# The way into the expert loop of an attention and mixture-of-experts kernel: an expert number loaded earlier on TensorE, three activation and residual pieces re-ordered, token loads in three buffers

## The reference

```python
x = x + xattn(layernorm(x), ctx)           # 16 heads of 32, 112 queries, causal mask
h = layernorm(x).reshape(T, H)
scores = softmax(h @ gate_weight.T)        # E = 8 experts
w, idx = top_k(scores, 2)
gu = einsum('th,efh->tef', h, gate_up)     # F = 352, gate and up together 704 wide
act = silu(gu[..., :F]) * gu[..., F:]
y = einsum('tef,te,ehf->th', act, combine(w, idx), down)
sgu = h @ shared_gate_up.T                 # a shared expert, Fs = 704
y = y + (silu(sgu[:, :Fs]) * sgu[:, Fs:]) @ shared_down.T
out = x + y
```

## Time and profile before

| | |
|---|---|
| time, median of 3 runs | 344.97 us (343.78 to 345.1) |
| the profiled execution's own time | 346.77 us |
| its span, first to last instruction | 345.0 us |
| TensorE busy | 327.2 us, 95% of the span |
| VectorE busy | 267.9 us, 78% |
| ScalarE busy | 233.1 us, 68% |
| GpSimd busy | 133.2 us, 39% |
| chain that ended last | PE 69%, ACT 10%, DVE 8%, DMA 6%, issue 3% |

### The profile page before, as it was taken

One profiled execution on the slowest core, in us unless ns is written; L12 is line 12 of the kernel. 1 busy time (PEld: TensorE's weight loads), 2 busy tenths in 40 slices (PEclk: granted clock), 3 DMA queues, 4 the chain that ended last, 5 costly groups with the idle time before them and its releaser, 6 DMA issues.

```text
span 345.0 us, 7024 instructions
## 1 busy us (share of the span) xinstructions
PE 327.2 (95%) x2285; PEld 281.6 (82%) x2285; DVE 267.9 (78%) x675; ACT 233.1 (68%) x582; POOL 133.2 (39%) x144
## 2 busy tenths in 40 slices
PE   7999979999999998999999899999999999999990
PEld 6898858777776786889898778889988998998980
DVE  4889757999936348855487999999998989999930
ACT  4666988999953232312326578898898889889830
POOL 4335464777844000164400007765742321231231
PEclk9999987999999999999999999999999999999996
DMA  7999300000002799994689953564455456455333
GB/s 232 378 341 379 110 1 3 3 2 1 3 2 95 289 357 327 430 327 152 217 253 236 299 179 82 96 135 101 84 117 130 84 89 138 103 89 120 71 42 50
DMA packets 31795, 53.01 MB, mean 154 GB/s; under 512 B 7440, under 2 KB 14992, under 8 KB 30736
## 3 DMA queue, kind: packets, MB, share of 16 engines
q1 hardware_dynamic: 27616, 43.34, 38.4%
q0 software_dynamic: 4144, 9.23, 14.9%
HBM read 32.22 MB, written 16.92 MB: 142 GB/s over the span
## 4 chain that ended last, share of the span: by engine, by line
PE 69%; ACT 10%; DVE 8%; DMA 6%; issue 3%; POOL 2%; POOLq 1%; SPq 0%; DVEq 0%; ACTq 0%
PE bank L554 26%; PE bank L877 21%; ACT prob L1038 5%; PE bank L901 5%; DMA out<-y_sb,dest 3%; PE bank L615 3%; PE bank L905 2%; PE bank L915 2%; PE bank L776 2%; PE bank L763 2%; PE bank L911 2%; DVE gu_parts L1279 2%; PE bank L546 2%; PE bank L626 1%; DMA w_sg<-sguT 1%
## 5 line engine op out<-in xcount | busy, mean ns | idle before, releaser
L533 POOL DMA_INDIRECT out<-y_sb,dest x21 | 38.4, 1830 | 114.9 <-DMA out<-y_sb,dest 68.1
L1279 DVE TENSOR_TENSOR gu_parts<-w_gu,gu_parts 128x704 fp32r<-128x704 f32 x84 | 77.0, 951 | 0.8 <-ACT gu_parts L993 0.4
L993 ACT ACTIVATE gu_parts<-w_gu 128x704 fp32r x84 | 66.2, 793 | 13.9 <-PE bank L877 12.3
L877 PE MATMUL bank<-gu_parts,xsT_hi 128*128 128x352 f32 x328 | 70.0, 335 | 1.4 <-DVE xsT_lo L1279 0.9
L877 PEld LDWEIGHTS bank<-gu_parts,xsT_hi 128*128 128x128 f32 x328 | 53.7, 188 | 8.8 <-issue 8.7
L877 PE MATMUL bank<-gu_parts,xsT_lo 128*128 128x352 f32 x164 | 39.7, 323 | 0.0
L554 PE MATMUL bank<-x2T_hi,w_sg_lo 128*128 128x512 f32 (+1 forms) x88 | 32.7, 372 | 0.2
L430 POOL TENSOR_TENSOR prob<-prob,rrow 112x448 f32<-112x448 f32 x30 | 27.5, 935 | 12.3 <-DVE rrow L1329 12.3
L554 PE MATMUL bank<-x2T_hi,w_sg_hi 128*128 128x512 f32 (+1 forms) x88 | 32.0, 363 | 0.0
L554 PE MATMUL bank<-x2T_lo,w_sg_hi 128*128 128x512 f32 (+1 forms) x88 | 31.9, 363 | 0.0
L506 POOL DMA_INDIRECT xs_dram<-x2n,slot_i x14 | 14.8, 1057 | 37.9 <-DVE eid L1574 33.9
(11 more groups left out here) (216 smaller groups left out, 830.8 us busy)
## 6 DMA issues: line engine op xcount, KB each, us to landing
w_gu<-guT SPq DMA_DIRECT2D x8, 1408.0 KB
xs_dram<-no_row SPq DMA_DIRECT2D x1, 5460.0 KB, 19.6
xs_in<-xs_dram SPq DMA_DIRECT2D x21, 256.0 KB, 4.5
w_dn<-dnT SPq DMA_DIRECT2D x8, 512.0 KB, 5.4
act_w<-act_e SPq DMA_DIRECT2D x19, 176.0 KB, 2.7
w_sg<-sguT SPq DMA_DIRECT2D x10, 256.0 KB, 5.4
w_dn<-dnT SPq DMA_DIRECT2D x8, 192.0 KB, 6.1
w_sd<-sdnT SPq DMA_DIRECT2D x5, 256.0 KB, 6.0
```

Source lines behind the costliest of these rows:

```text
L533: pool.indirect_dma_start(out=out[:, :], out_offset=bass.IndirectOffsetOnAxis(ap=dest[:, i, 0:1], axis=0), in_=y_sb[i % 2][:, :], in_offse ...
L877: ins = pe.matmul(dst[:, 0:F], xsT[x_][:, c, :], gu2[w_][:, c, f0:f0 + F], start=c == 0 and n == 0, stop=c == C - 1 and n == 2)
L993: act.activation(dst, src, ACT.Copy).then_inc(s[sem], 1)
L1279: dve.tensor_tensor(lo_, src, hi_.bitcast(F32), ALU.subtract).then_inc(s[sem], 1)
```

## The change

There are six edits, and all lie at the entrance of the expert loop or in it.

1. TensorE loads the number of the first tile's expert (`e_first`) ahead of `shared_down(ND-1, 0)`, together with the wait for `pos`, and no longer between chunk 0 and chunk 1 of `gate_up(1)`. The other tiles load theirs where they did.
2. TensorE waits for `xs_lo` of tiles 1 to 20 ahead of the third pair of products of chunk 0, and no longer ahead of the first.
3. VectorE's last three additions are spread: two stood ahead of `gu_lo` of tile 1 and one behind `dn_lo(0)`. Now the first is behind `gu_lo(1, 0)`, the second behind `gu_lo(1, 2)` and the third behind `aT_lo(0)`.
4. `xs_in` is three buffers. Token tile 2 has one of its own (in the place of `y_sb0`), the even tiles from 4 on one at the end of the shared region, and tiles 0, 1 and the odd ones the old one. `load_x(2)` is issued right behind the late down weights.
5. On SP's queue `act_words` of tile 0 stands ahead of the first `start_sum`. The second `start_sum` stands behind `act_words` of tile 1. `load_x(i+3)` stands behind `act_words` of tile i, where `load_x(i+2)` stood ahead of it.
6. On ScalarE `put_y(18)` stands ahead of `dn_hi(19)` and not behind it.

```diff
--- before.py
+++ after.py
@@ -164,6 +164,7 @@
     actT_split = pair(loop, "actT_split", [P, 2, P])
     actT_plain_at = loop[0]
     actT_plain = m.inside(loop, "actT_plain", [P, P])
+    y0_at = loop[0]
     y_sb = [m.inside(loop, "y_sb0", [P, H])]
 
     parts = [shared_at, shared_end]
@@ -182,7 +183,8 @@
                nc.alloc_sbuf_tensor_at("dn_last_lo", [P, (E - 1) * H], F32R, offset=dn_last_lo_at))
 
     sb = lambda name, shape, dtype=F32: m.inside(small, name, shape, dtype)
-    xs_in = sb("xs_in", [P, XW])
+    xs_in = [sb("xs_in", [P, XW]), nc.alloc_sbuf_tensor_at("xs_in1", [P, H], F32, offset=shared_end - 4 * H),
+             nc.alloc_sbuf_tensor_at("xs_in2", [P, H], F32, offset=y0_at)]
     no_row = nc.alloc_sbuf_tensor_at("no_row", [P, XW], F32, offset=act_p_at)
     ident_f = sb("ident_f", [P, P], F32R)
     negmax = sb("negmax", [SQ, R, C])
@@ -259,8 +261,10 @@
 
         "sg ssil sact sact_hi sact_lo sdn sres "
 
-        "xin Tx xs_hi xs_lo gu_hi gu_lo dn_hi dn_lo eg esil eact actw Ta aT_hi aT_lo aT dn_last_hi dn_last edn_split edn ey yst").split()
+        "xin0 xin1 xin2 Tx xs_hi xs_lo gu_hi gu_lo dn_hi dn_lo eg esil eact actw Ta aT_hi aT_lo aT dn_last_hi dn_last edn_split edn ey yst").split()
     s = {n: nc.alloc_semaphore(f"s_{n}") for n in names}
+
+    token_buffer = lambda i: 2 if i == 2 else 1 if i > 2 and i % 2 == 0 else 0
 
     with nc.Block() as block:
 
@@ -341,7 +345,7 @@
 
 
             def load_x(i):
-                sp.dma_start(xs_in[:, 0:H], xs_dram[bass.ds(i * P, P), 0:H]).then_inc(s["xin"], 16)
+                sp.dma_start(xs_in[token_buffer(i)][:, 0:H], xs_dram[bass.ds(i * P, P), 0:H]).then_inc(s[f"xin{token_buffer(i)}"], 16)
 
             for e in range(0, 2):
                 load_gu(e, s["wegu"])
@@ -374,28 +378,32 @@
             for e in range(E - n_late, E):
                 load_dn(e, s["wedn_late"])
 
+            load_x(2)
+
             def start_sum(n0, n1):
                 sp.dma_start(tiles_of(out, n0, n1), xres[:, n0:n1, :]).then_inc(s["ysum0"], 16)
 
+            def act_words():
+
+                sp.dma_start(act_w[:, :], act_e[:, :]).then_inc(s["actw"], 16)
+
+            sp.wait_ge(s["eact"], 1)
+            act_words()
+            sp.wait_ge(s["Tx"], 2)
+            load_x(3)
             sp.wait_ge(s["sres"], NX * ND - XB[1] + 1)
             start_sum(0, BLK + 1)
-            sp.wait_ge(s["Tx"], 2)
-            load_x(2)
-
-            def act_words():
-
-                sp.dma_start(act_w[:, :], act_e[:, :]).then_inc(s["actw"], 16)
-
-            sp.wait_ge(s["eact"], 1)
-            act_words()
-            sp.wait_ge(s["sres"], NX * ND)
-            start_sum(BLK + 1, NX)
             for i in range(1, NT - 2):
-                sp.wait_ge(s["Tx"], i + 2)
-                load_x(i + 2)
                 sp.wait_ge(s["Ta"], i)
                 sp.wait_ge(s["eact"], i + 1)
                 act_words()
+                if i == 1:
+                    sp.wait_ge(s["sres"], NX * ND)
+                    start_sum(BLK + 1, NX)
+                    sp.wait_ge(s["sdn"], NX * ND)
+                if i + 3 < NT:
+                    sp.wait_ge(s["Tx"], i + 2)
+                    load_x(i + 3)
 
             sp.wait_ge(s["yst"], 16 * NT)
             sp.wait_ge(s["ysum0"], 16 * 3)
@@ -770,11 +778,12 @@
 
 
             def t_x(i, bank_=S[2]):
-                pe.wait_ge(s["xin"], 16 * i + 16)
+                own = token_buffer(i)
+                pe.wait_ge(s[f"xin{own}"], 16 * sum(token_buffer(n) == own for n in range(i + 1)))
                 pe.wait_ge(s["idf"], 1)
                 for c in range(C):
                     ins = pe.transpose(bank_[:, c * P:(c + 1) * P].bitcast(F32R),
-                                       xs_in[:, c * P:(c + 1) * P].bitcast(F32R), ident_f[:, :])
+                                       xs_in[token_buffer(i)][:, c * P:(c + 1) * P].bitcast(F32R), ident_f[:, :])
                 ins.then_inc(s["Tx"], 1)
 
             out_bank = (B, CC, D, A)
@@ -860,6 +869,8 @@
             pe.wait_ge(s["sact"], NBLK * (ND - 1) + 1)
             t_x(0, S[1])
             shared_gu(ND, 1)
+            pe.wait_ge(s["pos"], 3)
+            e_first = pe.value_load(eid[0:1, 0:1], min_val=0, max_val=E - 1)
             shared_down(ND - 1, 0)
             shared_down(ND - 1, 1, slice(0, XB[1] - 1))
 
@@ -868,11 +879,14 @@
 
                 if chunks[0] == 0:
                     pe.wait_ge(s["xs_hi"], i + 1)
-                    pe.wait_ge(s["xs_lo"], i + 1)
+                    if i == 0:
+                        pe.wait_ge(s["xs_lo"], 1)
                 for c in chunks:
                     pe.wait_ge(s["gu_hi"], C * i + c + 1)
                     pe.wait_ge(s["gu_lo"], C * i + c + 1)
                     for n, (x_, w_) in enumerate(((0, 1), (0, 0), (1, 0))):
+                        if c == 0 and x_ == 1 and i > 0:
+                            pe.wait_ge(s["xs_lo"], i + 1)
                         for dst, f0 in ((S[0], 0), (S[1], F)):
                             ins = pe.matmul(dst[:, 0:F], xsT[x_][:, c, :], gu2[w_][:, c, f0:f0 + F],
                                             start=c == 0 and n == 0, stop=c == C - 1 and n == 2)
@@ -956,11 +970,10 @@
             t_x(1)
             shared_down(ND - 1, 1, slice(XB[1] - 1, None))
             pe.wait_ge(s["sres"], NX * ND - XB[1] + 1)
-            pe.wait_ge(s["pos"], 3)
             for i in range(1, NT - 1):
                 pe.wait_ge(s["eact"], i)
                 gate_up(i, range(1))
-                e = expert(i - 1, lowest=int(i > SPLIT_FROM))
+                e = expert(i - 1, lowest=int(i > SPLIT_FROM)) if i > 1 else e_first
                 gate_up(i, range(1, C - 1))
                 if i == NT - 2:
                     e_last = [expert(n, lowest=1) for n in (NT - 2, NT - 1)]
@@ -1251,8 +1264,10 @@
                     act.wait_ge(s["wedn"], 16 * 2 * (E - n_late))
                     act.wait_ge(s["wedn_late"], 16 * 2 * n_late)
                     act.wait_ge(s["dest"], 16)
+                if i == NT - 2:
+                    put_y(i - 1)
                 dn_hi(e, i)
-                if i >= 1:
+                if 1 <= i < NT - 2:
                     put_y(i - 1)
                 if i == NT - 2:
                     put_actT(i)
@@ -1623,26 +1638,29 @@
                     xs_lo(0)
                 add_shared(ND - 1, 0, c, c + 1)
                 gu_lo(e, 0, c)
-            add_shared(ND - 1, 1, 0, 2)
             for i in range(NT):
                 if i + 1 < NT:
                     e_next = expert(i + 1)
-                    for c in range(2):
-                        gu_lo(e_next, i + 1, c)
+                    gu_lo(e_next, i + 1, 0)
+                    if i == 0:
+                        add_shared(ND - 1, 1, 0, 1)
+                    gu_lo(e_next, i + 1, 1)
                 if i == NT - 1:
                     dn_lo(e, i)
                 elif i >= 1:
                     aT_lo(i - 1)
+                if i == 1:
+                    add_shared(ND - 1, 1, 2)
                 expert_act(i)
                 if i + 1 < NT:
                     xs_lo(i + 1)
-                    for c in range(2, C):
-                        gu_lo(e_next, i + 1, c)
+                    gu_lo(e_next, i + 1, 2)
+                    if i == 0:
+                        add_shared(ND - 1, 1, 1, 2)
+                    gu_lo(e_next, i + 1, 3)
                     dn_lo(e, i)
                 if i >= NT - 2:
                     aT_lo(i)
-                if i == 0:
-                    add_shared(ND - 1, 1, 2)
                 e = e_next
 
 
```

4 lines of the change are left out of this document (2 added, 2 removed).

## The result

The changed kernel takes 344.13 us in the median (341.52 to 347.2), the kernel before 346.11 (343.78 to 349.19), 20 executions each; the ratio is 0.9942, with a 95% interval of 0.9922 to 0.9963. That is 2.0 us less (1.3 to 2.7), where I forecast 3.0. The time of 344.13 lies just above my range, which ended at 344.0. Of the 2.1 between 342.0 and 344.13 some 1.1 is the baseline (344.97 came from three executions, twenty gave 346.11) and 1.0 is the change.

A forecast was written before the change was run, and what follows sets the result against it. TensorE was taken to bound the loop, a row of accumulating DMAs the end. Gains of 1.7 (entrance), 0.9 (late tiles), 0.2 (copies) and 0.2 (end) sum to 3.0: from 344.97 to 342.0, range 341.0 to 344.0.

The forecast's parts named there:

- the entrance: Start of the expert loop on TensorE: low products of the first down come 1.7 earlier, bounds 1.0 and 1.8.
- The load: TensorE's expert number in tile 1: moving it lets chunk 1 follow chunk 0 at once, saving 0.68.
- the low part: Tile 1 on TensorE: chunk 0 needn't wait for `xs_lo` ahead of its first product; 0.3 to 0.4 at the loop's start.
- the additions: VectorE ahead of tile 1: one addition instead of two starts `act_e` at about 195.47 instead of 195.91, 0.44 earlier.
- the queue order: SP's queue: the first `act_w`, issued ahead of large transfers, lands in 2.1 to 2.7; at 4.4, 1.3 would be lost.
- edit 2 in the late tiles: Tiles 11 to 19 on TensorE: the later wait for `xs_lo` saves 0.1 each, 0.9 in all, bounds 0 and 1.0.
- edit 6: End of the kernel: ScalarE's `y_sb` of tile 18 starts 0.3 earlier; 0.2 counted, bounds -0.5 and 0.9.
- The price: Last tile: `dn_hi(19)` and `dn_lo(19)` come about 0.7 later, delaying TensorE some 0.6, covered by the row of DMAs.
- the moved second sum: SP's queue: issued at about 203.5 instead of 200.4, costed at nothing unless the first accumulation starts from 209.0 on.
- the 208: Accumulating DMAs: the forecast is wrong if the first accumulation starts after 208.
- the copy: Activation copies in the loop: issued ahead of the rows, they are late less often; gain 0.2, between 0 and 1.4.
- my first rival: Loop start: VectorE or a late `act_w` limits the gain to 0.7 instead of 1.7; total 2.0, time 343.0, chance 0.22.
- the third of my signs of being wrong: End of the kernel: the forecast is wrong if TensorE's last tile pushes the last accumulation.

The follow-up runs named there:

- after_again: The changed kernel run once more with no edit, for a second trace: 344.10 us, ratio 0.994 to the kernel before.
- old_put_y: The changed kernel with ScalarE's `dn_hi` of the last tile ahead of `y_sb` of tile 18 again: 346.58 us in a single execution.
- splits_later: The changed kernel with GpSimd's third-down-block splits moved from behind the accumulations of tiles 0 and 1 to tiles 2 to 7: 344.80 us, ratio 0.9946.
- early_and_later: low_part_first with GpSimd's splits moved as in splits_later, the first only behind the accumulation of tile 2: 343.80 us, ratio 0.9924.
- second_sum_early: The changed kernel with VectorE's last addition at the end of tile 0 and the second sum ahead of the second `act_w`: 343.28 us, ratio 0.9935.
- low_part_first: second_sum_early with VectorE's `aT_lo(0)` ahead of the second `gu_lo` of tile 2 instead of behind it: 343.35 us, ratio 0.9929.
- low_wait_first: The changed kernel with every tile waiting for the low part of its rows ahead of its first product again: 345.45 us, ratio 0.9983.
- old_queue: The changed kernel with SP's order of sums, rows and `act_w` from before, the three buffers kept: 346.50 us, ratio 1.0003.
- after: The first trace of the changed kernel, no edit: 344.74 us in the profiled execution, median 344.13, ratio 0.9942.

## Why the prediction was right and wrong

**Right in its mechanism: the entrance.** The load, the low part, the additions and the queue order each did what was forecast, and each undone alone loses it again. From S to the first transposes the changed kernel takes 3.14 (after_again; 3.93 in the first trace, where a packet met the first copy) instead of 4.98 to 5.06, which is 1.9 (1.7 forecast). `aT_lo(0)` ends 5.85 behind S, which is 201.9 on the clock of the trace of before, as worked out. The parts, each undone alone: load 0.48 (0.68 forecast), additions 0.34 (0.44), low part 0.94 (0.3 to 0.4), queue order 2.4 (1.3). They add up to 4.2 and not to 1.9, since undoing one brings back a wait that hid or was hidden by another.

**Right, and a little small: edit 2 in the late tiles.** 59.75 and 59.87 became 58.52, so 1.2 in nine tiles, 0.14 each, for 0.9 forecast. The piece of 18 products fell from 3.02 to 2.85, below the 2.91 that I took as its floor.

**Right in size, not in mechanism: edit 6.** It gave some 0.35 for 0.2, but not because `y_sb` of tile 18 comes earlier: the accumulation's issue is shorter, as old_put_y shows. I hadn't seen that. The price came as forecast: TensorE waits 0.9 for `dn_lo(19)` where it waited 0.26, under the cover of the row of DMAs.

**Wrong: the moved second sum.** These terms come to 3.5 or so. The step that failed is in the part on edits 4 and 5, "The second one is now issued at about 203.5 instead of 200.4. Accumulation for tile 0 waits for it, and it has `y_sb` of tile 0 some 1.7 earlier", which I costed at nothing, with 209.0 as the point from which it decides. I had asked only whether the accumulations could catch up, and not beside what. They did catch up. But against S the first one starts 12.3 and 11.7 behind instead of 11.05, while TensorE is 1.1 and 1.9 ahead. On the clock of the trace of before that is 208.3 and 207.8: the first is past the 208 that I had named as a sign of being wrong, and both are short of 209.0. The next come 5.6 and 5.9 apart instead of 6.2 and 7.2. GpSimd's splits come with them, and in tile 2 they fall on both of VectorE's pairs (3.06 and 2.35) instead of one. TensorE stands 0.6 to 0.7 for `aT_lo(2)`, its loader 1.1. The third copy takes 3.7 to 3.9, but TensorE doesn't stand for it in these two traces. Tiles 0 to 4 lose 1.0 on the means (28.42 of the two traces against 27.45). splits_later and early_and_later show the part of the splits: with them moved, the stop for `aT_lo(2)` is gone. second_sum_early shows that of the sum: with it early again, the periods behind the first are as before the change.

**Wrong in sign: the copy.** I counted a gain of 0.2 for late copies. The DMA did become faster, 2.07 in the median instead of 2.7. But in each trace one to four of the later copies meet a code packet and land 0.7 to 2.4 later, of which TensorE feels up to 0.8 each. The two traces of before have one such copy each. The trace of the changed kernel lost about 1.4 between tiles 9 and 18 to it and 0.8 at the first copy; after_again 0.1. How often on the whole, 16 traces don't tell. "The first `act_w` landing in 2.1 to 2.7" held in ten of the 13 traces with the new queue.

**The base.** The forecast time was taken off 344.97, the median of three executions. Off 346.11, that of twenty, the same 3.0 would have given 343.1. So 1.1 of the distance from 342.0 to 344.13 says nothing of the mechanism; the other 1.0 does.

**The account.** 1.9 + 1.2 + 0.4 = 3.5; less 1.0 in tiles 0 to 4; less 0 to 2 by late copies. That is 0.5 to 2.5, and the two traces have 0.8 and 2.5 against the mean of the two of before, 149.3. The measured 2.0 lies in it, but so would many values. The total is that of my first rival (2.0 instead of 3.0), and half of its reason, but not at the place that I gave: not `aT_lo(0)` but `aT_lo(2)`. That its number fits is luck.

**The other signs.** From tile 2 on the accumulations are released by ScalarE, as I said; in the first trace of before, 17 were by a DMA. The last one is released by ScalarE's `y_sb` too (the row at 336.64 under old_put_y), where before it was by the DMA. So TensorE's last tile does reach it, the third of my signs of being wrong, but it costs 0.1 at most: it starts 0.83 behind the landing of the one before, and 0.75 is the least in these traces.

**The chances.** Faster by more than 0.5% came true, by a narrow margin (0.58%, and the interval reaches down to 0.37%).

**What stays open.** Why VectorE gives way in one case and GpSimd in the other wasn't tried out. No version removed both the stop and its causes: second_sum_early, low_part_first and early_and_later have ratios 0.1% to 0.2% below the changed kernel's, taken in other sessions, which their intervals don't tell from nothing. So the stop is explained where it arises, but that removing it makes the whole kernel faster is not shown.

## What to carry to other kernels

When a transfer is moved back because "it is needed only later", look at what is released by it and then runs to catch up: its helpers (here GpSimd's splits) come closer together and meet other work. A copy on the critical path should have more to spare than its usual landing time; here it varied by a factor of two. And when a gain of 2 in 345 is to be explained, cut the traces at the same events: the code ahead of the change varied by 2.9 between executions.

## What the runs showed of the hardware

- GpSimd and VectorE hold each other up on some instructions. Beside a split, a pair of subtractions from two SBUF operands takes up to 3.06 instead of 1.68; the subtraction with an operand in PSUM (`xsT_lo`, 0.69) isn't slowed. The Trainium skill ("SBUF — State Buffer", SBUF: two separate sides) describes this as an exclusive lock on a shared pair of ports, for GpSimd against VectorE with two SBUF inputs. The trace agrees, and the accumulation that kept GpSimd 4.02 beside an unslowed pair looks like the same from the other side.
- A code packet of 16384 bytes that starts within the first 1.6 us of a copy of 176 KB delays it by 0.7 to 2.4, although it has only a tenth of its bytes (32 of 32 such copies; without one the median is 2.07).
- Loading a register on TensorE takes 0.30 in the median of every trace, below the 0.6 that the prediction quotes as a floor; the measurement decides. The first load of a trace takes 0.49 to 0.50, and 1.154 and 1.180 in the two traces of before, beside a transfer of 1.3 MB. In ten of the 13 traces with the new queue order one or two more are long, 0.64 to 1.10, most of them 2.1 to 4.6 behind the start of the first accumulation. The longest, in low_wait_first, makes that period 7.24 instead of some 6.73; so such loads are a part of the spread in tiles 0 to 4.
- TensorE's granted clock fell from 1.0 to 0.50 (2.4 to 1.2 GHz) in an idle time of 2.26 (old_queue), and not at idle times of 0.64 (after) and 1.58 (splits_later). The fall lasted 3.4 and cost some 0.9.
